# A four-layer image network on one core: first image of the attention taken with both query halves first, stacked on chip, its value transposes moved into a wait

## The reference

```python
x = x + L0(_gn(x))   # Volterra 3x3 convolution, first and second order (54 tap pairs)
x = x + L1(_gn(x))   # 3x3 convolution (flipped, all input channels summed), by FFT in the reference
x = x + L2(_gn(x))   # below
x = x + L3(_gn(x))   # two-dimensional Hartley transform, a mix of channels per mode, back

# L2, cut: token and query image xin, first pair of four; h is zero, so that the
# pairs with h leave constants (a mean over window sums in one case)
xin = einsum('nchw,oc->nohw', x, W_in) + b_in
q = conv(xin, Wq, 'SAME').reshape(n, 4, 8, 1024)     # heads x 8 channels x queries
k = conv(xin, Wk, 'VALID').reshape(n, 4, 8, 900)     # keys
v = conv(xin, Wv, 'VALID').reshape(n, 4, 8, 900)
w = softmax(einsum('nhcq,nhcd->nhqd', q, k), axis=-1)
a = einsum('nhcd,nhqd->nhcq', v, w)
# pre = projections of the attentions + gate biases; i, f, o = sigmoid, g = tanh
# hout = sigmoid(pre_o) * tanh(i * g);  out = W_out hout + b_out
```

## Time and profile before

| | us |
|---|---|
| median of 3 runs (321.5 to 324.03) | 322.73 |
| the profiled execution | 322.51 |
| its span, first to last instruction | 320.5 |
| PE busy | 285.3 (89%) |
| DVE busy | 209.8 (65%) |
| ACT busy | 180.6 (56%) |
| POOL busy | 34.3 (11%) |
| mean granted clock of TensorE | 0.946 |

### The profile page before, as it was taken

One profiled execution on the slowest core, in us unless ns is written; L12 is line 12 of the kernel. 1 busy time (PEld: TensorE's weight loads), 2 busy tenths in 40 slices (PEclk: granted clock), 3 DMA queues, 4 the chain that ended last, 5 costly groups with the idle time before them and its releaser, 6 DMA issues.

```text
span 320.5 us, 10448 instructions
## 1 busy us (share of the span) xinstructions
PE 285.3 (89%) x4522; PEld 133.7 (42%) x4528; DVE 209.8 (65%) x476; ACT 180.6 (56%) x346; POOL 34.3 (11%) x42
## 2 busy tenths in 40 slices
PE   5999979799987499999999999999989799896981
PEld 2577523234332144534444455444434232243670
DVE  3992172577279424789788887888878322249985
ACT  1301101125167377989899898988969788330510
POOL 9400000010000000010010100101020010620000
PEclk9999999999798556999999999999999999999897
DMA  7100000004688539700000000000000000000001
GB/s 262 49 4 4 4 11 0 3 0 110 186 173 114 141 111 262 333 33 3 4 2 5 2 3 4 2 4 4 2 4 2 4 3 0 2 0 4 3 4 65
DMA packets 3472, 15.43 MB, mean 48 GB/s; under 512 B 731, under 2 KB 1547, under 8 KB 2883
## 3 DMA queue, kind: packets, MB, share of 16 engines
q1 hardware_dynamic: 3171, 14.67, 16.5%
q0 software_dynamic: 256, 0.11, 0.2%
HBM read 12.21 MB, written 2.37 MB: 45 GB/s over the span
## 4 chain that ended last, share of the span: by engine, by line
PE 61%; DVE 17%; issue 9%; DMA 6%; ACT 3%; POOL 3%; DVEq 0%; ACTq 0%; POOLq 0%
PE ps L1179 12%; PE ps L1197 11%; PE ps L1150 10%; PE ps L1039 9%; DMA arena_a<-mt_sb 6%; PE ps L1098 4%; ACT arena_b L675 2%; PE ps L1301 2%; PE ps L1086 2%; DVE sums L884 2%; PE ps L1009 2%; PE ps L1254 2%; PE ps L1074 2%; DVE mx L889 1%; PE ps L1203 1%
## 5 line engine op out<-in xcount | busy, mean ns | idle before, releaser
L675 ACT ACTIVATE arena_b<-ps 128x512 f32<-128x512 f32 x232 | 124.9, 606 | 25.1 <-PE ps L1179 23.7
L1179 PE MATMUL ps<-arena_a 75*32 75x512 bf16 x896 | 90.6, 394 | 6.6 <-DMA arena_a<-mt_sb 5.9
L1150 PE MATMUL ps<-arena_a 72*32 72x450 bf16 x1024 | 92.7, 377 | 1.0 <-DVE vrest L854 0.8
L889 DVE TENSOR_REDUCE mx<-ps 128x1 f32<-128x450 f32 x120 | 68.5, 616 | 2.3 <-PE ps L1150 2.1
L884 DVE CUSTOM_DVE_ANT_0 sums<-ps,relus 128x450 bf16<-128x450 f32 x68 | 41.3, 625 | 34.4 <-PE ps L1150 28.4
L1197 PE MATMUL ps<-arena_b,vt 128*32 128x512 f32 x448 | 60.5, 610 | 1.5 <-ACT arena_b L675 1.0
L1179 PEld LDWEIGHTS ps<-arena_a 75*32 75x32 bf16 x896 | 26.4, 98 | 51.4 <-ACT arena_b L675 21.6
L1150 PEld LDWEIGHTS ps<-arena_a 72*32 72x32 bf16 x1024 | 30.5, 101 | 38.7 <-issue 14.4
L683 ACT ACTIVATE relus<-ps 128x450 f32<-128x450 f32 x68 | 37.3, 552 | 6.6 <-PE ps L1150 6.5
L1039 PE MATMUL ps<-arena_a,cst 32*32 32x512 f32 x864 | 28.6, 596 | 0.8 <-ACT arena_a L626 0.8
L1009 PE MATMUL ps<-zeros 128*128 128x512 bf16 x78 | 21.5, 417 | 7.2 <-DMA xa<-x 3.5
(11 more groups left out here) (143 smaller groups left out, 229.4 us busy)
## 6 DMA issues: line engine op xcount, KB each, us to landing
arena_b<-wmodes SPq DMA_DIRECT2D x1, 4096.0 KB, 20.1
arena_a<-k_scratch SPq DMA_DIRECT2D x3, 516.8 KB
arena_a<-q_scratch SPq DMA_DIRECT2D x3, 384.0 KB
cst<-consts SPq DMA_DIRECT2D x1, 1045.0 KB, 9.7
k_scratch<-arena_b SPq DMA_DIRECT2D x3, 344.5 KB, 3.7
cst<-consts SPq DMA_DIRECT2D x1, 864.5 KB, 7.7
arena_a<-k_scratch SPq DMA_DIRECT2D x6, 129.2 KB
arena_a<-k_scratch SPq DMA_DIRECT2D x3, 258.4 KB
```

The source lines that it names most:

```text
L675: nc.scalar.activation(probs[:, n % PRING, :], ps[:, SCORE_RING[n % len(SCORE_RING)], :], ACT.Exp).then_inc(expd, 1)
L889: nc.vector.tensor_reduce(mx[:, a, e:e + 1], bank, AX.X, ALU.max).then_inc(max_read, 1)
L1150: last = mm(ps[32 * j:32 * j + 32, block_bank(i), 0:KHALF], qst[0:PAIR_ROWS, e, g, q0:q0 + 32], kst[0:PAIR_ROWS, g, at:at + KHALF], start= ...
L1179: last = mm(ps[32 * j:32 * j + 32, bank, :], kst[0:S_ROWS, g, k0:k0 + 32], qst[0:S_ROWS, e, g, :], start=True, stop=True)
```

## The change

It has more parts than its short name:

- **Start.** POOL clears `vt` and `vrest` after its first reciprocal root, not before; their ones are set there too. L0's halves are column halves (18 and 16 of 34 columns of the maps) in place of row halves. DVE empties half 0, waits for its sum, transposes, adds and measures it, and then does the same for half 1; PE issues both sums (`add_taps`) after the last tap matmul. The second normalisation is written in two pieces, rows 0 to 13 and the rest, and the first plane matmuls wait for the first piece only.
- **x_in** is computed in 32x32 tiles (`c_("win")[rows, rows]`) in place of 128x32, in the order of row shifts, with other banks.
- **Q, K, V** are convolved in the order Q0, K0, K1, Q1, V0, V1 (halves), and ACT and DVE split them in that order. The bias addition to `xb`, `ident_b` and the start value of `mx` leave DVE's part there (the last two go to POOL).
- **Stacking.** Image 0 is stacked from `q_parts` and `k_parts` on chip: SP takes query heads 0 and 1, POOL heads 2 and 3; of the 12 key transfers of the first and difference columns (`KDIFF` = 0, now in front) each takes 6; the second key columns follow. Q1 is written to DRAM by POOL and read back by SP (`q_second`). The other images still go through DRAM, written by POOL after `q_second`; SP reads image b after the b-th turned maxima have landed (`m_in`, 16 b), and the second queries of images 1 to 3 after the fourth. `wm` waits for all eight.
- **Order of halves**: (0,0), (1,0), (0,1), (0,2), (0,3), (1,1), (1,2), (1,3) as (e, b). The first two halves are all pairs, as before.
- **Fillers**: after each pair of half 0 but the last, and after each of the nine pairs of half 1 that run ahead, PE runs four 32-column matmuls on 256 columns of zeros (`keep_clock_tiled`).
- **Value transposes** come after half 0's last block, while DVE splits the maxima; ACT copies them. Half 0's turn is not moved behind four blocks.
- **Window sums** are made by POOL in 18 additions after the second turn; their matmuls, the bias addition and the gate constants come in the last half, and gates, cell, hidden and output of piece 0 two steps later.

The diff, cut to its core:

```diff
+HALVES = ((0, 0), (1, 0), (0, 1), (0, 2), (0, 3), (1, 1), (1, 2), (1, 3))
+EARLY_RING = (3, 4, 5, 7, 0, 2)
+SP_FIRST = ((0, 0), (0, 2), (1, 1), (2, 0), (2, 2), (3, 1))
+POOL_FIRST = ((0, 1), (1, 0), (1, 2), (2, 1), (3, 0), (3, 2))
...
+            if s == 0 and a < ROWS_OF_MAX - 1:
+                stream.append(("fill", 256))
         stream.append(("split", s))
+        if s == 0:
+            stream += [("vt", 0), ("vt_copy", 0), ("vt", 1), ("vt_copy", 1)]
         stream.append(("turn", i, s))
...
-    take(2 * ROWS_OF_MAX + 1 + FIRST_AHEAD)
+    take(2 * ROWS_OF_MAX + 1)
+    for _ in range(FIRST_AHEAD // 2):
+        take(2)
+        plan.append(("fill", 256))
...
-                    later += [(step + 1, ("gates", 0)), (step + 2, ("cell", 0)), (step + 3, ("hidden", 0)),
-                              (step + 4, ("out", 0))]
+                    later += [(step, ("window", "mean")), (step, ("bout",)), (step + 1, ("window", "value")),
+                              (step + 2, ("window", "gate")), (step + 3, ("gates", 0)), (step + 4, ("cell", 0)),
+                              (step + 5, ("hidden", 0)), (step + 6, ("out", 0))]
... sync
+            def stack_q_head(g):
+                for s in range(PARTS):
+                    sp.dma_start(qst[part_rows(s), 0, g, :],
+                                 q_parts[HC * g:HC * (g + 1), s, 0:HALF].unsqueeze(1).to_broadcast([HC, PARTS, HALF])
+                                 ).then_inc(q_head[g], 16)
+            def stack_k_head(g, s, cols, signal):
+                sp.dma_start(kst[part_rows(s), g, cols], k_parts[HC * g:HC * (g + 1), :, cols]).then_inc(signal, 16)
...
+            for g in range(2):
+                stack_q_head(g)
             for s in range(PARTS):
                 sp.wait_ge(k_part[s], 2)
+            for g, s in SP_FIRST:
+                stack_k_head(g, s, K_FIRST, k_head[g])
...
+            for s in range(PARTS):
+                stack_k_head(0, s, K_SECOND, k_second)
+            sp.wait_ge(qd_written[1], PARTS * 16)
+            stack_q(1, 0, HEADS, q_second)
+            for s in range(PARTS):
+                stack_k_head(1, s, K_SECOND, k_second)
             sp.wait_ge(kd_written, PARTS * 16)
             sp.wait_ge(qd_written[0], PARTS * 16)
+            for b in range(1, B):
+                sp.wait_ge(m_in, 16 * b)
+                stack_k(b)
+                stack_q(0, HEADS * b, HEADS * (b + 1), q_in[b - 1])
+            sp.wait_ge(m_in, 16 * B)
+            stack_q(1, HEADS, G, q_in_second)
... gpsimd
+            for g in range(2, HEADS):
+                for s in range(PARTS):
+                    pool.dma_start(qst[s * PARTS * HC:(s + 1) * PARTS * HC, 0, g, :], ...).then_inc(q_head[g], 16)
+            for s in range(PARTS):
+                pool.wait_ge(k_part[s], 2)
+            for g, s in POOL_FIRST:
+                stack_k_part(g, s, K_FIRST, k_head_pool[g])
+            for s in range(PARTS):
+                pool.wait_ge(q_part[s], 2)
+                pool.dma_start(q_dram[s, 1].rearrange("c g n -> g c n"), q_parts[:, s, HALF:HW]).then_inc(qd_written[1], 16)
+            for s in range(PARTS):
+                pool.wait_ge(k_part[s], 3)
+            for g in range(2, HEADS):
+                for s in range(PARTS):
+                    stack_k_part(g, s, K_SECOND, k_second_pool)
+            pool.wait_ge(q_second, PARTS * 16)
+            for s in range(PARTS):
+                pool.dma_start(k_dram[:, s, HEADS:].rearrange("c g n -> g c n"), k_parts[32:P, s, :]).then_inc(kd_written, 16)
+            for s in range(PARTS):
+                pool.dma_start(q_dram[s, 0, :, HEADS:].rearrange("c g n -> g c n"), q_parts[32:P, s, 0:HALF]
+                               ).then_inc(qd_written[0], 16)
             for item in plan:
                 if item[0] == "turn":
...
+                    if s == 1:
+                        window_sums()
... vector, in the loop over the two halves of L0
                 for b in (1, 3):
+                    nc.vector.tensor_copy(l0q[:, b, half], ps[:, 2 * b + e, :]).then_inc(l0_evac_dve, 1)
+                dve.wait_ge(first_loaded, 16)
+                dve.wait_ge(l0_summed, e + 1)
+                nc.vector.transpose(...)
+                nc.vector.scalar_tensor_tensor(xb[:, half], l0t[:, half], c_("l0bias"), xa[:, half], ALU.add, ALU.add)
+                link(nc.vector.bn_stats(stats[:, 6 * e:6 * e + 6], xb[:, half]))
... tensor
+            def keep_clock_tiled(bank, n):
+                for j in range(COL_TILES):
+                    mm(ps[32 * j:32 * j + 32, bank, 0:n], zeros[:, 0:32], zeros[:, 0:n], start=True, stop=True)
...
+            for e in range(2):
+                pe.wait_ge(padded, 4)
                 for r in range(3):
+                    for b in range(B):
+                        rows = slice(32 * b, 32 * b + 32)
+                        last = mm(ps[32 * r:32 * r + 32, XIN_BANKS[e * B + b], :].rearrange("p (y x) -> p y x", x=W),
+                                  c_("win")[rows, rows], window(xp[rows], r, 1, 16 * e, 16, W), start=True, stop=True)
...
+            conv(Q_BANKS[0], qkv[:, 0], H, W, 0, q_done, 0)
+            conv(K_BANKS[0], qkv[:, 1], KH, KH, 1, k_done, 0)
+            conv(K_BANKS[1], qkv[:, 1], KH, KH, 1, k_done, 1)
+            conv(Q_BANKS[1], qkv[:, 0], H, W, 0, q_done, 1)
+            conv(V_BANKS[0], qkv[:, 2], KH, KH, 1, v_done, 0)
+            conv(V_BANKS[1], qkv[:, 2], KH, KH, 1, v_done, 1)
```

More of the change, by code:

```diff
@@ L416, in build, with in_list @@
         plan = attention_plan()
-        prologue = 2 * ROWS_OF_MAX + WIDE_AHEAD
+        def in_list(parts, head):
+            return sum(g == head for g, _ in parts)
         def block_bank(i):
-            ring = SCORE_RING + MAX_RING if i < prologue else MAX_RING
+            last = 2 * ROWS_OF_MAX
+            ring = EARLY_RING if i < last else AHEAD_RING if i < last + 1 + FIRST_AHEAD else MAX_RING
             return ring[i % len(ring)]
@@ new lines, in _ @@
+            act.wait_ge(k_done, 1)
+            nc.scalar.activation(k_first, ps[:, K_BANKS[0], 0:KHALF], ACT.Copy).then_inc(k_copied, 1)
+            act.wait_ge(k_copied, 1)
+            k_copy(0, first, k_first)
+            act.wait_ge(k_left, 1)
+            k_copy(1, first, k_res[:, first])
+            act.wait_ge(k_left, 2)
+            k_copy(0, diff, k_res[:, diff])
+            act.wait_ge(k_done, 2)
+            k_copy(0, second, ps[:, K_BANKS[1], 0:KHALF])
+            act.wait_ge(k_left, 3)
@@ L852, in _ @@
-            for h in range(HEADS):
-                r = slice(32 * h, 32 * h + KREST)
-                nc.vector.tensor_copy(vrest[r, :, 32 * h:32 * h + HC],
-                                      ps[r, 1, 3 * P:4 * P].rearrange("p (b h c) -> p b h c", h=HEADS, c=HC)[:, :, h, :]
-                                      ).then_inc(vt_ready, 1)
+            first, diff, second = (slice(KEY0, KEY0 + KHALF), slice(KDIFF, KDIFF + KHALF), slice(KEY0 + KHALF, KEY0 + KEYS))
+            dve.wait_ge(q_part[0], 1)
@@ new lines, in conv @@
+            def conv(bank, weights, rows, cols, first, signal, e):
+                ny = rows // 2
+                for px in range(3):
+                    for b in range(B):
+                        last = mm(ps[32 * b:32 * b + 32, bank, 0:ny * cols].rearrange("p (y x) -> p y x", x=cols),
+                                  weights[:, px, :], window(xst[:, b, :], first, first + px, ny * e, ny, cols),
+                                  start=(px == 0), stop=(px == 2))
+                last.then_inc(signal, 1)
@@ L1202, in values @@
                     for h in range(HEADS):
[L1203 removed]
+                        last = mm(ps[32 * h:32 * h + 32, bank, :], vrest[:, HALVES[half][1], 32 * h:32 * h + 32],
                                   probs[:, n0 % PRING, :], start=False, stop=True, skip_group_check=True)
```

591 lines of the change are left out of this document (342 added, 249 removed).

## The result

The changed kernel took 305.97 us at the median of 4 runs (304.95 to 308.1), beside 322.87 us for the kernel before (321.5 to 324.03, 4 runs): ratio 0.949, 95% interval 0.942 to 0.955. On a second chip it took 306.22 us against 322.57 (ratio 0.951, 0.947 to 0.954). The profiled execution had 308.1 us over a span of 306.3; its mean clock was 0.971, against 0.984 to 0.990 in the other three runs.

What follows compares the result with a forecast made beforehand. It saw a ladder of single steps from 59.98 to 111.97 us, then PE and ACT together as bound. Terms -14.7 + 0 + 1.5 = -13.2 took 322.5 to 309.3, stated as 309.5 us; range 307 to 312 (wider 300 to 319).

Steps and rivals of the forecast that it cites:

- The forecast's own case: Whole kernel: 309.5 us, range 307 to 312, with the clock falling in half 0 of the scores; chance 0.42.
- rival (a): Half 0: the clock holds, -6.2 us, with +1 for image 1's stack; total 304 us (301 to 307), chance 0.28.
- +0.3 forecast: Start to x_in: -0.4 + 1.05 - 0.35 = +0.3 us, so the x_in convolution begins at T = 60.3.
- +1.05: End of the first stage: DVE's half-by-half order takes 7.7 us against 6.6, a loss of 1.05 us.
- of which I count -0.35: Before x_in: plane matmuls start once the first 14 rows are normalised, 0.45 us possible, 0.35 counted as gain.
- T + 17.4 forecast: First maxima block: starts 17.4 us after x_in's start (T), at 77.7 instead of 90.6.
- T + 37 forecast: First score: 37 us after x_in's start (T), set by POOL's 27 transfers; 97.3 against 111.97, -14.7 us.
- at most 5 us from T + 28.3, and then idles for some 3 us: Before the first score: PE's nine pairs ahead finish within 5 us, then PE idles some 3 us.
- (b): POOL's queue: issues cost 1.2 us each, first score 8 us later, total 318 us; chance 0.18 shared with another rival.
- (c): POOL's queue: the gain is gone at 1.45 us an issue; at 1.6 the end is at 326; chance 0.07.
- I therefore expect the clock to fall here too: Half 0 of the scores: a PE hole drops the clock, so it takes 25.4 us again, change 0.
- +1.5 forecast: Last half: window matmuls and DVE's bias addition move in, +1.5 us (0 to 3.0); a dip could add 1.6.

Runs made afterwards that it cites:

- run 2: Changed kernel with 14 matmuls of 512 columns on zeros between layer 0's two tap sums, DVE order kept: 305.51 us, ratio 0.947 to the kernel before.
- run 1: Changed kernel, but DVE empties half 1 of layer 0 before it sums half 0: 302.61 us, ratio 0.938 to the kernel before.
- run 3: Changed kernel without the filler matmuls on zeros among the first maxima blocks: 310.21 us, ratio 0.963 to the kernel before.
- Run 11: Changed kernel with SP alone issuing all 24 head transfers of the first image's stacks: 320.29 us, ratio 0.987 to the kernel before.
- Run 6: Changed kernel with POOL's six DRAM writes of q and k issued behind the first turn: 307.89 us, ratio 0.951 to the kernel before.
- run 9: Changed kernel with seven pairs ahead instead of nine, half 1 emptied first in layer 0, six DRAM writes behind the first turn: 316.28 us, ratio 0.976.
- run 12: Changed kernel with the value transposes right before the first score instead of in the split's hole: 318.65 us, ratio 0.984 to the kernel before.
- run 4: Changed kernel with one of the nine taps of the window value sum, eight left out: 308.15 us, ratio 0.949 to the kernel before.
- Run 7: Changed kernel with SP no longer waiting for turned maxima before stacking images 1 to 3: 312.59 us, ratio 0.963 to the kernel before.
- run 10: Changed kernel with half 1 of layer 0 emptied first and 16 equal columns per window matmul instead of one: 302.72 us, ratio 0.935.

## Why the prediction was right in its total, and where not

**The total** of 309.5 stands 3.5 us above the median, inside the range. The forecast's own case (307 to 312) did not come; rival (a), the clock holds, gave 304 and comes nearer. The profiled execution, 2.1 us above the median, shows how it came about: against the forecast it had +2.8 at the start, +1.2 and -1.8 up to the first score, -5.2 in half 0 and +1.9 in the last half. Errors of several us cancel in it, so that the closeness of the total is in part luck.

**Start (+0.3 forecast, +3.1 measured).** The order on DVE was seen, and priced at +1.05 from durations alone. It was mis-sized: the last statistics end at 47.8 against 45.24 before, +2.55. From the start of the first tap sum to that end it takes 6.7 us before, 8.3 in run 2, where the clock holds, and 9.2 here: the order alone costs 1.6, and the clock 0.9 more. The terms ahead of the taps cancelled: the first stage began 1.0 us earlier (9.02 for 10.02, forecast 0.4) and took 29.6 us in 16-wide pieces where it took 28.6, a term I had at nothing with a bound of +1.5. The +2.55 all lies behind them, round the 3.84 us hole of PE between the two tap sums. I had listed the hole's pieces and not asked of the clock what I asked of it two stages later; it fell, and taps 1.06 us long took 1.93. The last 0.6 us are the term "of which I count -0.35". The plane matmuls begin 3.1 us behind the statistics instead of 2.5, although they wait for the first rows alone: at half clock the 14 matmuls on zeros of L1178 took 5.19 us and stood in their way to 50.98. Where the clock was back in time (runs 1, 2 and 3) the distance is 2.33, a gain of 0.2.

**x_in and the first maxima (T + 17.4 forecast, T + 18.6 measured).** The tiles took 2.21 us for the forecast 1.6. PE was through with V1 at 80.9; the block then waited 0.85 us for the head's last key transfer, a landing of 3.9 us where 2.7 was taken. SP's key issues were priced at 0.38 us from its reads of DRAM; these on-chip ones came 0.7 us apart and more (5.78 us for the first six). Run 11 bears out that a second queue is to be priced by its issues: 4 us, with the clock on top.

**The first score (T + 37 forecast, T + 36.4 measured).** The number was right, but the chain that it was built on ended second. I built it from POOL's 27 transfers, six writes last. (Its sum takes T + 22.3 for 18.8 + 3.2 = 22.0 and 5.2 for six issues of 0.9; the two slips nearly cancel.) The second queries were back at T + 27.6, as forecast. POOL's issues took 0.55 to 0.58 us each for the 96- and 128-row writes too, where 0.9 was taken, so the queue was clear at 94.1, and the turned maxima landed at T + 35.6. Run 6 took the writes away and left the 6.28 us between maxima and score as they were; run 9 took two pairs away and shortened them by 1.55. The nine pairs, forecast as hidden ("at most 5 us from T + 28.3, and then idles for some 3 us"), began at T + 29.9, took 6.3 us and end last. Rivals (b) and (c) needed 1.2 and 1.45 us an issue; no issue of POOL's took more than 0.8 here.

**Half 0 (0 forecast, -5.2 measured).** The step that failed is "I therefore expect the clock to fall here too". It rested on an idle of 3 us before the first score, and there is none, because of the pairs. What holds the clock are two parts of the change, each shown alone: the fillers (run 3, 5 us) and the transposes in the split's hole (run 12, some 5.5 to 7 us). Rival (a)'s -6.2 + 1 is the measured -5.2, but not by its reasoning: its +1 was to come from image 1's stack, and PE waited for no transfer from 99 to 144 us. The first two steps took 2.84 us for 2.51, and PE's waits there are for ACT's exponentials. The cited rule, the Trainium skill, TensorE: Matmul & The Clock Gate, "Part 4: PE-mode transpose", says that transposes do not count as busy in the same way. By it the seven PE-mode transposes should not have held the clock in the hole. Moving them let it fall, but eight of the fifteen records moved are ordinary matmuls on an identity, so the trace does not say which of them held it.

**The last half (+1.5 forecast, +1.74 without and +3.4 with a fall).** The term was sized right, and so was the possible dip of 1.6 us for this profile; others had more. Of the ten profiles with the whole chain in its place, seven had the fall, the changed kernel's first among them, and it costs 1.6, 3.2 or 4.9 us. That the one-column matmuls bring it is not shown. Why it comes in one run and not in another stays open. The 4 MB transfer was under way in both cases, and run 4 with one tap held the clock beside it in its profiled execution.

**Pacing** was forecast to shorten turn 1's landing, "and PE hardly waited for it". Run 7 shows its worth: without it that landing is 10.95 us and PE waits 4.1. Image 1's stacks behind the first turn cost nothing, since PE never waited for them; read 0 to read 6 is unchanged to 0.1 us.

A loss of the change that the runs show is the order in layer 0. Undone (runs 1 and 10) it gives 302.6 to 302.7 us, ratio 0.935 to 0.938.

## What to carry to other kernels

Ask of every hole on PE that a change makes or fills what the clock does behind it: here holes of 2.4 to 4.8 us cost up to some 7 us more than themselves, and two cheap coverings (zero matmuls between blocks, transposes that had to be done anyway) decided the 5.2 us of half 0, where the forecast looked at a queue. When two chains end at nearly the same time, price both, the one that you take for hidden too; the first score waited for work that was "ahead". And work that runs ahead is a lead that all later halves live on: cutting it brings the first result sooner and the last one later.

## What the runs showed of the hardware that was not expected

- POOL's issue of a transfer took 0.55 to 0.61 us on average, alike for the 24-row stacks and the writes of 96 and 128 rows (3.37 and 3.64 us for six, 1.65 to 1.73 for three).
- The first stage's 864 fp32 matmuls of the same total columns took 29.6 us where the moving operand is read in 16-wide pieces, 28.6 with 32-wide ones; each half is 0.5 us longer, and PE has no idle time in it.
- Matmuls with 1 and with 16 fp32 columns took the same: 72 in 2.15 us both times.
- During a fall PE reads as fully busy (16 us of 86 to 102 at 15.58 busy in run 3): only the clock column shows that time is lost.
- A DMA of 12 KB took 10.95 us beside the stacks in run 7 and 2.1 to 4.6 us in the changed kernel, which holds those back; its 4.6 are the first turn's behind six writes, and 2.5 with the writes moved (run 6).
